# Cross attention on one core: the weighted values of a tile and the scores of the next change places in TensorE's order

## What is computed

```python
xq = _layernorm(result, ln2_g, ln2_b)
xs = _layernorm(src, ln2_g, ln2_b)
kv = xs @ ed_wkv
k2, v2 = (_heads(t) for t in jnp.split(kv, 2, axis=-1))
q2 = _heads(xq @ ed_wq)
wei2 = jnp.einsum('bhtd,bhjd->bhtj', q2, k2) * scale
wei2 = jax.nn.softmax(wei2, axis=-1)
ed_out = _merge(jnp.einsum('bhtj,bhjd->bhtd', wei2, v2)) @ ed_wproj + ed_bproj
```

## Time and profile before

| | us |
|---|---|
| median of three runs | 1438.62 |
| lowest and highest | 1436.42, 1440.64 |
| the profiled execution, by the same clock | 1435.06 |
| its span in the profile | 1433.3 |
| TensorE busy | 1186.2 |
| VectorE busy | 1008.1 |
| ScalarE busy | 744.6 |
| GpSimd busy | 730.5 |

### The profile page before, as it was taken

One profiled execution on the slowest core, in us unless ns is written; L12 is line 12 of the kernel. 1 busy time (PEld: TensorE's weight loads), 2 busy tenths in 40 slices (PEclk: granted clock), 3 DMA queues, 4 the chain that ended last, 5 costly groups with the idle time before them and its releaser, 6 DMA issues. The chain is left out here.

```text
span 1433.3 us, 38489 instructions
## 1 busy us (share of the span) xinstructions
PE 1186.2 (83%) x15852; PEld 760.5 (53%) x15852; DVE 1008.1 (70%) x1819; ACT 744.6 (52%) x1021; POOL 730.5 (51%) x1047
## 2 busy tenths in 40 slices
PE   3888836898989999999999999897496977869784
PEld 2555523555555555555556565554343746347472
DVE  5677765787888888888888787876456373774733
ACT  2333332567676767666676767675333425234150
POOL 2345648646455555555464646420068394783940
PEclk9999957999999999999999999999987999989995
DMA  7100013232313132313132222110000000000000
GB/s 177 49 0 0 0 33 120 79 100 66 112 59 112 64 109 69 109 56 121 58 99 80 95 83 86 58 49 20 16 0 2 1 7 3 0 6 0 6 0 6
DMA packets 70383, 75.66 MB, mean 53 GB/s; under 512 B 21308, under 2 KB 64956, under 8 KB 70108
## 3 DMA queue, kind: packets, MB, share of 16 engines
q1 hardware_dynamic: 70236, 73.58, 16.7%
HBM read 32.91 MB, written 0.92 MB: 24 GB/s over the span
## 5 line engine op out<-in xcount | busy, mean ns | idle before, releaser
L916 DVE TENSOR_REDUCE tops_sb<-ps_b 112x2 f32<-112x1000 f32 x384 | 460.0, 1198 | 130.2 <-PE ps_b L777 130.0
L878 ACT ACTIVATE probs_sb<-ps_a 128x896 f32<-128x896 f32 x352 | 322.6, 916 | 91.5 <-PE ps_a L758 91.5
L749 PE MATMUL ps_d<-probs_sb,values_sb 128*32 128x112 f32 x6144 | 226.8, 265 | 1.0 <-ACT probs_sb L878 1.0
L777 PE MATMUL ps_b<-keys_sb,queries_sb 64*112 64x500 f16 x768 | 162.6, 419 | 69.2 <-DVE tops_sb L916 63.7
L217 POOL TENSOR_SCALAR context_sb<-context_sb,ln_sb 125x128 f32<-125x128 f32 x384 | 166.4, 450 | 7.9 <-POOL ln_sb L235 7.8
L226 POOL TENSOR_TENSOR ln_sb<-st_sb 125x12 f32<-125x12 f32 x32 | 7.2, 223 | 308.4 <-DVE st_sb L960 283.0
L749 PEld LDWEIGHTS ps_d<-probs_sb,values_sb 128*32 128x32 f32 x6144 | 134.1, 109 | 40.2 <-issue 6.7
L758 PEld LDWEIGHTS ps_a<-queries_sb,keys_sb 64*128 64x128 f16 x3072 | 123.7, 103 | 52.4 <-ACT probs_sb L878 9.0
L777 PEld LDWEIGHTS ps_b<-keys_sb,queries_sb 64*112 64x112 f16 x768 | 49.6, 124 | 186.9 <-DVE tops_sb L916 120.9
L758 PE MATMUL ps_a<-queries_sb,keys_sb 64*128 64x112 f16 x3072 | 139.8, 210 | 6.2 <-ACT probs_sb L878 6.0
L1087 POOL TENSOR_TENSOR turn_b_sb<-turn_b_sb,const_sb 128x512 f32<-128x512 f32 x64 | 83.0, 1297 | 98.0 <-DVE turn_b_sb L1422 98.0
(11 more groups left out here) (253 smaller groups left out, 2019.3 us busy)
## 6 DMA issues: line engine op xcount, KB each, us to landing
keys_sb<-k_split_sb SPq DMA_DIRECT2D x288, 125.0 KB, 3.0
context_sb<-in_ctx SPq DMA_DIRECT2D x32, 750.0 KB
queries_sb<-q_split_sb SPq DMA_DIRECT2D x24, 112.0 KB, 5.5
keys_sb<-in_ones SPq DMA_DIRECT2D x3, 375.0 KB, 4.8
w_qk_sb<-in_w_qkv SPq DMA_DIRECT2D x1, 1024.0 KB, 11.5
queries_sb<-shift_sb SPq DMA_DIRECT2D x64, 1.8 KB
x_all_sb<-in_x SPq DMA_DIRECT2D x2, 448.0 KB
queries_sb<-in_zeros SPq DMA_DIRECT2D x8, 112.0 KB, 5.5
```

What stands on the lines that cost most here:

```text
L749: last = nc.tensor.matmul(o_bank[32 * (g % 4):32 * (g % 4) + 32, 112 * (g // 4):112 * (g // 4) + 112], values[r][:, k, g, :], probs[k % 2] ...
L777: last = nc.tensor.matmul(ps_b[0:2 * T, 512 * e:512 * e + 500], queries_of(b + d, e, g), keys[(r + d) % 3][64 * e:64 * e + 64, g, 500 * u: ...
L878: nc.scalar.activation(probs[s % 2][:].rearrange("p (e n) -> p e n", e=2), halves(ps_a[:, :]), ACT.Exp).then_inc(Q["probs_ready"], 1)
L916: nc.vector.tensor_reduce(tops[(b + d) % 2][:, :, n // 3, n % 3], ps_b[0:2 * T, :].rearrange("p (e n) -> p e n", e=2)[:, :, 0:500], axis=A ...
```

## The change

In the steps 1 to 11 the scores of tile s and the products of tile s-1 change places in TensorE's queue. The wait of the scores for `probs_ready` is no longer written, since the products, now ahead, wait for the same count. Step 0, the other engines and all transfers stay as they are.

```diff
@@ -791,13 +791,12 @@
                                                  start=True, stop=True).then_inc(Q["k_done"], 1)
                             if has(d):
                                 scan(UNITS[s], d)
-                            if s > 0 and has(0):
-                                wait("probs_ready", 0, s)
-                                scores(b, r, s)
                             if s == 0 and has(-1):
                                 pv(-1, KT - 1, r2, wait)
                             if s > 0 and has(0):
                                 pv(0, s - 1, r, wait)
+                            if s > 0 and has(0):
+                                scores(b, r, s)
                             if b == 0 and s == 0:
                                 pe.wait_ge(cleared, 15)
                             if s == 0 and has(0):
```

## The result

The changed kernel takes 1497.01 us (median of four runs, 1495.1 to 1497.68), the kernel before 1438.46 beside it. The ratio is 1.041, with a 95% interval of 1.0394 to 1.0427. The profiled execution took 1496.48 us, its span is 1494.7 us, 61.4 more than before. The forecast was 1493, in a range of 1474 to 1520.

The account below looks back on a forecast made before the run. No engine was taken as full: VectorE's 1.72 us cycle bounds bare steps, TensorE those with stages, exp the last element. Adding 44.2, 4.25 and 5.8, all 54.2 us, to the kernel before gave 1493 us, range 1474 to 1520.

Parts of the forecast that it names:

- The removed wait frees nothing: Scores' wait in steps 1 to 11: costed at zero, since the products already waited for the same exp.
- Prices of the new order: Start-to-start times: scan to products 0.35, products to scores 0.52, scores to exp 0.42, scores to next stage 0.30 us.
- TensorE's step +0.10: Steps with a key or values stage: from 1.07 to 1.17 us, as scan and scores no longer overlap.
- exp cycle 1.91: Products to products through signal, scores and exp: 1.91 us instead of 1.38, above VectorE's 1.72.
- Steps 3 and 4: A bare step, then a values step: 3.88 us before, 4.17 after, +0.29 per element.
- Step 7 to step 0: End of each element: last exp +1.09 us later, 0.29 given back before xs_t, so +0.80.
- Clock: TensorE's granted clock in the last element: a fall costed at nothing; if it fell, 7 us more.
- Element 0: Steps 1 to 6 of the first element, up to its scan 7: +0.70 us.
- The sum: Whole kernel: 44.2 us up to scan 7 of element 29, then +4.25 and +5.8, all 54.2 us.
- Part of the cover: Rival: scores overlap the products ahead by 0.17 us, products to scores 0.42, cycle 1.81; 1457 us, 5%.
- weights loaded ahead: Rival: scores' weights pass the products, scores start 0.30 us behind them, cycle 1.69; 1424 us, 3%.
- a dearer boundary: Rival: scores to the next stage costs 0.47 us, +0.17 at seven places per element; 1528 us, 4%.

Follow-up runs that it names:

- busy_steps: Kernel before, with the new order only in steps 1, 2, 4, 5 and 6 of elements 0 to 29: 1453.86 us, ratio 1.0113.
- bare_steps: Kernel before, with the new order only in steps 3 and 7 to 11 of elements 0 to 29: 1468.04 us, ratio 1.0212.
- lag_two: Kernel before, with products ahead of scores but taken from the tile before the last, so they wait for an older exp: 1456.00 us, ratio 1.014.
- clock_fill: Changed kernel plus an unread 300-column matmul behind the scores in each step of the last two elements: 1486.94 us, ratio 1.0351 to the kernel before.
- tail_only: Kernel before, with the new order only in the last two elements: 1455.96 us, ratio 1.0132.
- values_halved: Kernel before, with each values stage cut into two halves, spread over steps 3 to 8: 1409.40 us, ratio 0.9808.
- halved_turn: values_halved with the transposes of the result moved from step 0 to step 3: 1428.28 us, ratio 0.9945 to the kernel before.
- body_only: Kernel before, with the new order in elements 0 to 29 and the old one in the last two: 1475.77 us, ratio 1.027.
- best_late: halved_stats in the order of the change: 1465.93 us, ratio 1.0202 to the kernel before.
- turn_three: Kernel before, with the transposes of the result moved from step 0 to step 3: 1426.13 us, ratio 0.9929.
- halved_stats: values_halved with the context statistics of step 7 moved to step 0: 1397.51 us, ratio 0.973 to the kernel before.

## Why the prediction was right

- *The removed wait frees nothing.* Right: the products wait in its place, 89 us on their weight loads.
- *Prices of the new order.* Scan to products 0.35, products to scores 0.52, scores to exp 0.41 (put at 0.42) and the unseen one, scores to the next stage, 0.30: all measured as put, so the way to the last (0.07 us before the modelled end of the stage ahead) held.
- *TensorE's step +0.10, exp cycle 1.91.* Right, and shown apart by busy_steps, bare_steps and lag_two. Steps 3 and 4: +0.29 forecast, +0.29 found.
- *Step 7 to step 0.* +0.80 forecast, 0.57 found by the scans. The path was wrong: I sent the delay through xs_t and its gaps, but o_wide waits for the products, 0.65 or 0.66 behind their start in both kernels, and the products moved by 0.59. I had also put a gap of 0.07 between exp and xs_t where they overlap; with the gap, xs_t would have bound. So an element costs 1.29 us in place of 1.49.
- *Clock.* This is the term that failed. I costed its fall at nothing and named 7 us for the last element. It fell there (5.8 us, 28.74 instead of 22.92), late in element 30 (about 1.2), in element 0 (about 1.4, below) and twice in the body, at 407.6 and 766.0, 1.4 us each:

```profile
403.00:407.47 4.47, 3.34 (x60) 1.81 (x58) 3.57 (x10) 2.67 (x4) 1.26 (x6) 1.00 0.02 4
407.47:410.88 3.41, 3.41 (x39) 2.09 (x43) 1.77 (x4) 1.68 (x2) 2.90 (x4) 0.51 0.00 0
```

- *Element 0* cost 2.3 us and not 0.7: its first products, at 262.23, take 0.97 us, as at half clock, which lasts to 264.2 here and to 260.8 in the kernel before. clock_fill, the same code up to there, has it to 261.3 and takes 15.69 us from scan 0 to scan 7 of element 0, where the kernel before takes 14.99: the forecast 0.70. So the rest is the clock; what holds it down longer in this trace is open.
- *The end.* The 1.5 us behind the cross attention, where both kernels are the same, no run explains: from the last products to the end the kernels here take 410.9 to 413.8 us, and tail_only, at half clock for its first 7.5 us, 411.9.
- *The sum.* The too high price of an element (29 × 0.2 = 5.8) offsets about half of the missing ones of the clock (about 11). That the time came out only 4 us above the forecast is in part luck: two errors of opposite sign.
- *Rivals.* Part of the cover (0.42 for products to scores), weights loaded ahead (0.30), and a dearer boundary (0.47 behind the scores) each named a number that the trace now shows otherwise. Of the two readings in the Trainium skill, TensorE: Matmul & The Clock Gate, the narrow one (The mechanism) fits for scores behind products: with no wait written between them the scores' weights still stood idle 0.17 us (526.34 in element 11, step 4).

## What to carry to other kernels

Before changing the order of two stages, follow the longest cycle that each of them closes: matmuls that wait for an exponential, put ahead of those that feed the next one, make the cycle longer by their whole length, and a share of 52% for ScalarE says nothing about it. Then check three things apart: neighbours on TensorE that overlap (0.17 us here), the slack of each step (0.34), and whether TensorE will stand idle long enough for its clock to fall. Idle time in bare steps is better filled by splitting a stage of the full ones, as long as the helper engine isn't made to wait in its own queue (0.35 us in values_halved, 0.59 in halved_turn).

## What the runs showed of the hardware

- The granted clock fell in the middle of a dense loop, behind a stretch in which TensorE was busy 3.34 of 4.47 us, and was back in the next stretch. It happened in 2 of the 28 elements in the middle of the changed kernel, one of bare_steps, two of clock_fill and none of body_only or best_late, each time in step 9, behind the bare steps 7 and 8. Each kernel has one trace. The Trainium skill, TensorE: Matmul & The Clock Gate, A second HAM failure mode: psum-queue depth-cycling, tells of such swings from frequent short idle times. The trace shows such swings, but body_only has the same idle times in its body and no fall, so why in these elements and not in the others stays open.
- In the last element, TensorE busy 11.48 of 17.13 us kept its clock in body_only, and 11.49 of 17.14 in the kernel before; as many matmuls, with the same exp cycle of 1.38 or 1.39 us, lost it for a part of the element in lag_two, turn_three, halved_turn and halved_stats. Work that nobody reads held it at 1.00 with TensorE busy 19.25 of 22.88 us.
- ScalarE starts xs_t 0.10 us before the exp ahead of it ends, in steps 9 and 10 of the changed kernel (57 times, for instance xs_t at 540.06 behind an exp of 539.25 that takes 0.92). The Trainium skill, ScalarE: Activation LUTs, What ACT_TABLE_LOAD costs, gives about 0.093 us for activations back to back; the trace agrees.
- Weights of the scores load 0.01 us behind the start of the scan, but 0.17 us behind the last load of the products, whether or not a wait is written between them (526.34 in the changed kernel; 542.65 in step 0, where waits are written).
